# Weight loads of a recommendation tower moved to ScalarE's queue, their splitting moved between the compares of the second half block

## The reference

```python
e = jnp.stack([tbl_0[ids[:, 0]], ..., tbl_26[ids[:, 26]]], axis=1)      # (2048, 27, 128)
interactions = jnp.einsum('bfd,bgd->bfg', e, e).reshape(B, F * F)
x = interactions[:, TRIL_IDX]                                            # 351 pairs
z = jnp.concatenate([bottom, x], axis=1)
h = jnp.concatenate([z, bottom], axis=1)                                 # 607 columns
h = jnp.maximum(h @ W_top1 + b_top1, 0.0)                                # 512
h = jnp.maximum(h @ W_top2 + b_top2, 0.0)                                # 256
y = h @ W_top3                                                           # 1
```

## Time and profile before

| | |
|---|---|
| median of 3 runs | 376.42 us (375.34 to 377.04) |
| the profiled execution, its device time | 379.08 us |
| its span in the profile | 377.3 us |
| TensorE busy | 351.3 us, 93% |
| GpSimd busy | 260.1 us, 69% |
| VectorE busy | 204.9 us, 54% |
| ScalarE busy | 140.9 us, 37% |

### The profile page before, as it was taken

The page is one execution under the profiler, slowest core; times in us unless marked ns, Lnnn a source line. Parts: engine busy times, 40 slices in busy tenths (PEclk is TensorE's granted clock), DMA queues, the critical chain, the costliest instruction groups (busy, mean ns, idle before and its releaser), DMA issues.

```text
span 377.3 us, 11203 instructions
## 1 busy us (share of the span) xinstructions
PE 351.3 (93%) x4420; PEld 332.2 (88%) x4420; DVE 204.9 (54%) x509; ACT 140.9 (37%) x243; POOL 260.1 (69%) x263
## 2 busy tenths in 40 slices
PE   3798969498899999999999999999999999999797
PEld 2787969497789998999999998999899998999785
DVE  4799456466048640984269542984078443972110
ACT  3445322325233353234333353225422443235332
POOL 5878777777777777777777777777777777871000
PEclk9999999699899999999999999999999999999899
DMA  7994347743427681456326552579337961841100
GB/s 205 243 249 123 110 135 210 146 118 77 137 58 160 116 151 49 123 133 140 94 54 174 115 134 55 126 130 137 91 81 151 123 128 50 146 116 42 36 2 0
DMA packets 37951, 44.01 MB, mean 117 GB/s; under 512 B 18855, under 2 KB 30266, under 8 KB 37928
## 3 DMA queue, kind: packets, MB, share of 16 engines
q1 hardware_dynamic: 29736, 26.92, 35.1%
q0 software_dynamic: 8192, 16.79, 17.3%
HBM read 38.48 MB, written 5.20 MB: 116 GB/s over the span
## 4 chain that ended last, share of the span: by engine, by line
PE 83%; SPq 5%; DVE 4%; DMA 4%; issue 3%; ACT 1%; DVEq 0%
PE ps_build L770 40%; PE ps_gram L808 12%; PE ps_dense L830 12%; PE ps_dense L856 7%; PE ps_build L794 3%; PE ps_gram L794 3%; DMA gram_dram<-gram 2%; SPq L376 2%; PE ps_dense L864 2%; DVE hot L463 1%; DVE table L434 1%; SPq L339 1%; PE ps_dense L785 1%; DMA id_raw<-ids_onehot_dram 1%; PE ps_gram L830 1%
## 5 line engine op out<-in xcount | busy, mean ns | idle before, releaser
L419 POOL DMA_INDIRECT rows<-tbl_dram,idx x256 | 259.3, 1013 | 79.6 <-issue 76.2
L770 PE MATMUL ps_build<-hot,table 125*128 125x256 f32 x1408 | 182.4, 288 | 11.3 <-DVE hot L463 5.3
L770 PEld LDWEIGHTS ps_build<-hot,table 125*128 125x128 f32 x1408 | 174.5, 195 | 14.5 <-DVE hot L463 5.8
L463 DVE TENSOR_SCALAR hot<-id_raw 125x512 fp32r<-125x512 f32 (+1 forms) x384 | 140.9, 421 | 18.9 <-PE ps_build L770 13.2
L578 ACT COPY embT<-ps_build 128x512 f32<-128x512 f32 (+1 forms) x48 | 38.1, 793 | 126.7 <-PE ps_build L770 126.7
L472 DVE COPY gram<-ps_gram 117x416 f32<-117x416 f32 x30 | 17.0, 586 | 76.7 <-PE ps_gram L808 76.7
L808 PEld LDWEIGHTS ps_gram<-embT 128*53 128x53 f32 x1920 | 48.6, 129 | 7.1 <-issue 5.8
L808 PE MATMUL ps_gram<-embT 128*53 128x52 f32 x1920 | 50.6, 213 | 2.8 <-issue 2.1
L830 PE MATMUL ps_dense<-pairT,w1p 125*128 125x256 f32 x270 | 37.6, 289 | 2.1 <-issue 2.1
L830 PEld LDWEIGHTS ps_dense<-pairT,w1p 125*128 125x128 f32 x270 | 34.7, 194 | 2.6 <-issue 2.2
L856 PE MATMUL ps_dense<-h,w2s 128*128 128x256 f32 x112 | 26.9, 393 | 0.0
(11 more groups left out here) (58 smaller groups left out, 139.7 us busy)
## 6 DMA issues: line engine op xcount, KB each, us to landing
id_raw<-ids_onehot_dram SPq DMA_DIRECT2D x35, 256.0 KB
gram_dram<-gram SPq DMA_DIRECT2D x60, 84.5 KB
raw<-tbl_dram SPq DMA_DIRECT2D x11, 448.0 KB
rows<-tbl_dram,idx POOLq DMA_INDIRECT x256
bot<-bottom_dram SPq DMA_DIRECT2D x8, 128.0 KB
id_raw<-ids_onehot_dram SPq DMA_DIRECT2D x7, 128.0 KB
w1p_raw<-w_pairs_dram SPq DMA_DIRECT2D x1, 750.0 KB
raw<-tbl_dram SPq DMA_DIRECT2D x11, 52.0 KB
```

What stands on the lines that cost most here:

```text
L419: nc.gpsimd.indirect_dma_start(rows[:, t, s * D:(s + 1) * D], None, tables[f], bass.IndirectOffsetOnAxis(idx[:, 2 * i + t, f:f + 1], 0)).t ...
L463: last = nc.vector.tensor_scalar(hot[0:VP, a % HOT_SLOTS, v, 0:w, :], shifted, float(v0 + v), None, ALU.is_equal)
L770: last = nc.tensor.matmul(bank[:, q * HALF:(q + 1) * HALF], table[0:VP, units[n][q], bits, row:row + D], hot[0:VP, a % HOT_SLOTS, v, q, :] ...
```

## The change

All weight loads leave SyncE's queue and go to ScalarE's. The three small ones (`w3`, `b1`, `b2`) stand ahead of everything else in ScalarE's program. The four large ones stand in half 0, after the copies of steps (0,1,0) and (0,1,1), with a wait for the last one-hot unit of half 0. In half 1 ScalarE makes the high part of `w1p` after unit 2 and no longer after unit 1, and waits for VectorE's low parts after unit 5 and no longer after unit 4. VectorE adds the two blocks after part 15, makes the low part of `w1p` after part 18 and that of `w1b` after part 22; before, it added after part 20 and made both low parts after part 23.

```diff
@@ sync @@
-            def load_weights():
-                for dst, src in ((w1b_raw[:, :], w_bottom_a), (w1b_more[:, :], w_bottom_b),
-                                 (w1p_raw[:, :, :], w_pairs.rearrange("(c p) h -> p c h", c=CHUNKS)),
-                                 (w2s[:, :, :], w2.rearrange("(c p) h -> p c h", p=128)),
-                                 (w3s[:, :], w3), (b1s[:, :], b1), (b2s[:, :], b2)):
-                    sp.dma_start(dst, src).then_inc(weights_in, 16)
...
             write_gram(0, 0)
-            load_weights()
             half(1, HALF)
@@ vector @@
-            def add_w1b():
...
-            def split_weights():
...
+            def split_weights(a):
+
+                if a == HOTS - 9:
+                    dve.wait_ge(weights_in, 16 * WEIGHT_LOADS)
+                    nc.vector.tensor_tensor(w1b_raw[:, :], w1b_raw[:, :], w1b_more[:, :], ALU.add).then_inc(w1b_added, 1)
+                if a == HOTS - 6:
+                    dve.wait_ge(weights_high, 1)
+                    low_part(w1p[:, LOW, :, :], w1p_raw[:, :, :], w1p[:, HIGH, :, :]).then_inc(weights_low, 1)
+                if a == HOTS - 2:
+                    dve.wait_ge(weights_high, 2)
+                    low_part(w1b[:, LOW, :], w1b_raw[:, :], w1b[:, HIGH, :]).then_inc(weights_low, 1)
...
                     make_hot(i, a)
...
-                    if is_half(i, FIRST + 1) and a == HOTS - 4:
-                        add_w1b()
+                    if is_half(i, FIRST + 1):
+                        split_weights(a)
                 if is_half(i, FIRST + 1):
-                    split_weights()
@@ scalar @@
+            def load_biases():
+                for dst, src in ((w3s[:, :], w3), (b1s[:, :], b1), (b2s[:, :], b2)):
+                    nc.scalar.dma_start(dst, src).then_inc(weights_in, 16)
+
+            def load_weights():
+
+                act.wait_ge(built, BUILDS * FIRST + nth("hot", len(units) - 1) + 1)
+                for dst, src in ((w1b_raw[:, :], w_bottom_a), (w1b_more[:, :], w_bottom_b),
+                                 (w1p_raw[:, :, :], w_pairs.rearrange("(c p) h -> p c h", c=CHUNKS)),
+                                 (w2s[:, :, :], w2.rearrange("(c p) h -> p c h", p=128))):
+                    nc.scalar.dma_start(dst, src).then_inc(weights_in, 16)
...
-                if n == 1:
+                if n == 2:
                     act.wait_ge(weights_in, 16 * WEIGHT_LOADS)
...
-                if n == 4:
+                if n == 5:
                     act.wait_ge(weights_low, 2)
...
             act.sem_inc(dense_act, acted(FIRST))
+            load_biases()
...
                 emb_tile(FIRST, 1, u)
+            load_weights()
             first_tile(FIRST)
```

More of the change, by code:

```diff
@@ L494, in pack @@
                 nc.vector.tensor_copy(*pack_rest(2)).then_inc(pack_dve, 1)
-            def add_w1b():
-                dve.wait_ge(weights_in, 16 * WEIGHT_LOADS)
-                nc.vector.tensor_tensor(w1b_raw[:, :], w1b_raw[:, :], w1b_more[:, :], ALU.add).then_inc(w1b_added, 1)
-            def split_weights():
[L503 to L506, removed]
+            def split_weights(a):
[8 more added lines that the diff above has]
+                    low_part(w1b[:, LOW, :], w1b_raw[:, :], w1b[:, HIGH, :]).then_inc(weights_low, 1)
             def half(i, more=True):
```

## The result

| | before | changed |
| --- | --- | --- |
| median of 20 runs, on one chip | 376.84 us (373.63 to 379.92) | 379.65 us (375.44 to 381.91) |
| ratio | | 1.0053 [1.0027, 1.0079] |
| profiled execution: time, span | 379.08, 377.3 | 379.83, 378.0 |

What follows compares the result with a forecast made beforehand. TensorE, 93% busy, was seen losing 9.24 us before step (1,1,1), with GpSimd's gathers limiting the gain to 6.50. Less 0.8 for the clock and 0.4 for the start: 5.3, so 376.42 becomes 371.1 us, range 368.3 to 374.8.

Steps and rivals of the forecast that it cites:

- What is late next: At step (1,1,1): its last gather ends at 80.14, rows land 1.64 later, so it starts at 81.78, gaining 6.50 us.
- second rival: Rows land late beside the weights, 4.94 us after the gather, at (1,1,1): gain 2.0 us, median 374.4; chance 18%.
- The slack of 2.7: In half 1 before (1,1,1): TensorE must wait 2.7 us for GpSimd anyway, so late landing in half 0 is harmless to that size.
- the sum: Whole kernel: gain 6.50 less 0.8 for the clock and 0.4 for the start, 5.3 us, giving a median of 371.1.
- The prediction's last sentence: Signs of error: late first gather, (0,1,2) or (0,1,3) holding TensorE over 3 us, (1,1,1) before 81, or GpSimd's pace changing.
- The rest of half 1 … I leave as it is: Half 1 behind (1,1,1), with its 2.11 us stop called issue: taken as unchanged, since its instructions are the same.
- 0.8 for the clock: After the new wait at (1,1,1): a lower clock costs 0.8 us, half of the 1.64 seen after the 5.13 wait.
- GpSimd's pace: First to last gather: GpSimd runs without a stop at its own pace, unchanged; last gather of (1,1,1) ends at 80.14.
- The range: Median: gain 4.5 to 6.9, so 369.5 to 372.3 for the forecast by itself; whole range 368.3 to 374.8.
- The new wait at (1,1,1): Ahead of step (1,1,1): TensorE waits 2.7 us for gathered rows, in place of the three old waits.
- the splits are covered: Half 1 before (1,1,1): moved splits hide in VectorE's lead, 0.5 us to spare; without it up to 1.75 comes back.
- the start costs: Kernel start: three small loads on ScalarE delay the first gather by one issue, 0.4 us, bounds 0 and 6.0.

Runs made afterwards that it cites:

- before_b: The kernel before, unchanged, profiled a second time; profiled execution 377.08 us.
- split_only_c: The kernel before with only the moved splits, all loads on SyncE's queue as before; ratio 1.0024 [0.9991, 1.0057].
- the two probes: Kernels with marker loads of 256 bytes timing when rows land, four large weight loads ahead of or behind the marks; total times are no verdict.
- sp_early_c: The change with the four large loads issued by SyncE instead of ScalarE, behind the same condition; ratio 1.0099 [1.0064, 1.0135] to the kernel before.
- again_b: The change as it is, run again with a second profile; ratio 1.0045 [1.0006, 1.0084] to the kernel before.
- third_early: As `late_c`, but two large loads (512 of 1,774 KB) stay at the change's early time; ratio 1.0013 [0.9984, 1.0042] to the kernel before.
- late_c: The change with the four large loads issued one step of the half later, still on ScalarE; ratio 1.0026 [0.9992, 1.006] to the kernel before.
- late_d: The same kernel as `late_c`, run again with a second profile; ratio 0.9993 [0.9958, 1.0028] to the kernel before.
- small_only: The kernel before with only the three small loads moved to ScalarE at the start; ratio 1.0004 [0.9971, 1.0037].
- late_old: The kernel of `late_c` with the splits of the kernel before; ratio 1.0006 [0.9971, 1.0041] to the kernel before.
- probe_without: The probe with the four large weight loads issued behind the marks; marks 2.80, 1.63, 1.57, 1.59 us after the last gather's end.

## Why the prediction was wrong

- **The step that failed is "What is late next".** It read the landing time, 1.64 us, off one place where nothing large travelled, and used it as a constant, and only at step (1,1,1). For half 0 the second rival said that a late landing "is harmless up to 2.7 us". It measured 5.86 at (0,1,3): 4.22 more. The 6.53 by which half 1 begins late are, in the order of the timeline, 0.13 from the start of the products at 44.03, 0.40 by the stop (2.46 in place of 2.06), 4.26 by steps (0,1,2) and (0,1,3) with the wait between them and transposes of 1.07 and 1.11 in place of 0.66, and 1.73 by the products at the lower clock (5.15 in place of 3.42). The slack of 2.7 takes 2.74 of it: 79.04 + 6.53 = 85.57, and step (1,1,1) began at 85.56 and not at the 81.78 of the sum. By the rival's own 4.94 the rows of (0,1,3) come 3.30 late, which is already more than 2.7; the text put the 4.94 at (1,1,1) only. The prediction's last sentence names a wait of more than 3 us at (0,1,3) as a sign of being wrong, and that is what came. The lower clock alone is no mark of the change: those products took 4.58 in `before_b` and 4.70 in `split_only_c`, with half 1 at 56.03 and 56.49. That rows land late beside the weights is shown by the two probes, by `sp_early_c` and `again_b` with the wait, by `third_early` with a part of it, and by `split_only_c`, `late_c` and `late_d` without it.
- **The rival was right in kind and too cheap.** The second rival named the weights travelling with the gather (0,1,3), but priced it at 4.94 us and let the slack of half 1 swallow it. The rule that it quoted, of the Trainium skill ("DMA: Bandwidth & Descriptors", section "Issuing engines are not separate DMA queues"), speaks against the change: loads of several engines interleave on the same DMA engines, and only the time of issue is saved. The runs agree: the rows land 5.92 us after their gather with the loads on SyncE, 5.86 and 5.99 with them on ScalarE.
- **"The rest of half 1 … I leave as it is" failed too.** Behind (1,1,1) the change loses 3.16, where the sum had 0.8 for the clock: 2.20 by the longer stop, and 0.96 by what runs at the lower clock after it (four products take 1.02 in place of 0.64). Beside `before_b`, which waits 1.61 us for rows in this stretch, the loss is 1.71. The longer stop comes with the splits, as `split_only_c` shows; why is not shown. It was absent where TensorE had just waited 5 to 8 us for rows (`late_c`, `late_d`, `third_early`), and near 2 where the old wait of 1.4 stood (1.75 and 2.11) and in `small_only`, where TensorE had lost time to a compare and a lower clock instead; `late_old`, with three waits of 1.48, 0.49 and 1.29 around, has none. It looks as if time lost ahead lets the supply of instructions catch up; that is argued only, and no run tests it.
- **The size of the gain was read from an untypical execution.** The sum took its 6.50 from 88.28; in `before_b` step (1,1,1) starts at 84.78, and the predicted 81.78 would have gained 3.0. The profiled execution lay 2.66 above the median, and the text noted that without asking where in the trace the 2.66 were.
- **GpSimd's pace was a second, smaller miss.** The gather that (1,1,1) needs ended at 81.62 and not at 80.14, since records of some gathers ahead of it were longer (one of 2.04 us at 78.32). With the gather ending there and 1.64 to land, the step would not have begun before 83.26, even with half 1 on time. The last gather of all began at 342.35 and not near 340.
- **The range was added up wrongly.** The ends that it names (clock 1.64 and 0, start 0.4 and 0) give a gain of 4.46 to 6.50, not 4.5 to 6.9, and 4.5 gives 371.9, not 372.3. The result lies outside either.
- **The new wait at (1,1,1) did not come, since half 1 came late itself;** TensorE reached it 3.94 us after its last gather. In `late_c` and `late_d`, where it could come, it did.
- **Right:** the ids follow the compare of unit 0 at once (62.88, with the half 6.53 late) and nobody waits for them; the splits are covered (TensorE at 84.75 finds the given vector ready), in part by luck, since half 1 itself was late: where it begins at 54.7 and 54.6, TensorE waits 0.74 (`late_c`) and 1.79 us (`late_d`) for compares beside the splits; the start costs 0.10 for the first gather (3.48 before); GpSimd still pauses 0.30 between gathers.

Open: what ends the stop called issue (the pages list a DMA queue called instruction, and no run tests whether the stops are waits for it); how much of the time lost is due to the late rows alone, since no version that removes them is faster than the kernel before, and the intervals of `again_b` and `late_c`, on one chip, overlap; and why late loads, with half 2 beginning 2.5 to 5.7 us earlier in `late_c` and `late_old` than in the kernels before, end level in the median. `late_old` starts half 2 at 104.06 and half 7 at 316.39, 212.33 later, where `late_c` needs 208.51; and the profiled execution of `late_c`, 374.51, is the fastest of its twelve. A trace is one execution, and executions of one kernel differ by some 6 us.

## What to carry to other kernels

When a load is moved to an earlier place, list every transfer with a reader close behind it in the new place as in the old: here 1.8 MB moved out of the way of one id load and into the way of a gather whose rows TensorE was already waiting for (0.28 us in the earlier trace rows). The time from a gather's end to its rows is no constant; read it where as much else travels as will travel after the change. And before a wait is counted as gain, look whether it stands in a second execution of the same kernel.

## What the runs showed of the hardware

- Rows of an indirect gather land 1.6 us after the gather's record ends on GpSimd when no large load travels (three of four marks of `probe_without`, 2.80 at the fourth), 2.57 with 0.5 MB of weights issued 3.6 us ahead of the gather (`third_early`), 3.25 to 5.99 with 1.8 MB, 5.3 to 8.0 where two id loads were issued shortly ahead of the gather's end (`late_c`, `late_d`, `third_early`). The record on GpSimd need not show it: 0.94 us at (0,1,3) in the change and before. Other gathers have records of up to 2.49 us (`late_old`).
- TensorE stops at the same instructions in most runs for a time called issue. Near 47 to 50 us it is 1.2 to 2.1 us where no large load travels (seven traces), and 2.3 to 3.7 where one does (`third_early` 2.33, changed 2.46, `again_b` 2.60, `sp_early_c` 3.70). In the probes, where SyncE's other loads wait, it is 0.66 with the weights and absent without them.
- A small load (`w3s`, `b1s`, `b2s`) takes 0.40 to 0.46 us of its queue at the start, and 0.60 to 3.58 behind 1.8 MB in the two executions of the kernel before.
- One chip (13 in the record) ran all kernels at 570 to 580 us twice, with stops called issue through the whole trace (89.9 us in one group). What sets it apart is not known.
